# Two attention phases on one core: order tables in pairs of half steps, whole TensorE jobs, and several small steps moved to other engines

## Chip, cores and metric

The kernel runs on one core of a Trainium2 chip. The metric is the device time of one execution in microseconds.

## What is computed

Eight sequences of 512 tokens with 256 features go through two layers. Each layer is an attention half and a feed-forward half, both modulated by a conditioning vector (shift s, scale c, gate g). Cut to what matters here:

```python
# layer 0
h = layernorm(x) * (1 + ca) + sa
q, k, v = h @ wq.T, h @ wk.T, h @ wv.T            # 16 heads of 16 features
q, k = rope(rms(q)), rope(rms(k))                 # per head, g_rms inside rms
y = softmax(q k^T / 4 + 1) v                      # per head
x = x + ga * (y @ wproj.T)
x = x + gb * ffn0(layernorm(x) * (1 + cb) + sb)   # ternary weights, scaled
# layer 1
h = layernorm(x) * (1 + ca) + sa
q, k, v = h @ Wq + bq, h @ Wk + bk, h @ Wv + bv
y = softmax(q k^T / 4) v                          # then normed per head, Wo, gate
x = x + ga * attn(y); x = x + gb * moe(...)       # experts
```

## The kernel before

The program is a row of stages: `setup`, `attention(0)`, `mlp0`, `attention(1)`, `experts`. The change touches `attention` alone. A batch is one sequence. Four heads form a group G, so a batch has four groups.

In `attention` every engine has a program of its own, written out as a loop over half steps `s`, with 64 half steps a batch (`SLOTS`). Each engine runs its instructions strictly in this order and waits on semaphores. Tables (`LAYER_NORM`, `PROJECT`, `ROTATE`, `STACK0`, `STACK1`, `AV_AT`, `STAGE_AT`) say in which half step a step of batch n stands. The steps that prepare batch n stand among the attention of the batches before it; for batches 0 and 1 they stand, in `EARLY0` and `EARLY1`, before the first exponential. Batch n starts at half step 64 n.

Every even half step, TensorE (lines 964 to 980) does two raw score matmuls into the two banks of `SM` (`raw`, 14 pairs ahead) and two score matmuls into one of two buffers `ST` (`scores`). The raw and the score matmuls use different row groups of the array. VectorE (`maximum`, line 678) takes the row maximum of each raw bank. The negated maxima of a group are transposed (job `MT`, line 820), copied by ScalarE (line 496), and put by a DMA of SyncE into the last row of `QS`, so that the exponential needs no other bias. ScalarE (`exponential`, line 487) turns two heads' scores into `P` with one instruction of 128x1024, on every odd half step. A value quarter multiplies `P` with `V`, float32, four heads side by side in 32-column groups of the array (`values`, line 918). A group has four quarters, and each is cut into two halves of 256 columns that stand in different half steps. The sums `AV` are copied to `ysb` (line 560), transposed back into the same bank (line 939), and divided on VectorE (`yn`, lines 708 and 714).

All other TensorE work is a job with the one bank `X`: transposes of the normalised tile (`T0`, `T1`), the projections `QK0` to `QK3`, `V0`, `V1`, transposes of the output (`YT`), in layer 0 the transposes of q and k high and low halves (`H0` to `H3`) and the output projection (`P0`, `P1`). Numbers are split into float16 high and low parts, so that a product takes three matmuls for each half of the features. A `QK`, `V` or `P` job stands in two pieces of two half steps. A job waits until the bank's last content has been read (`job_out`).

Around it, in order of the steps of one batch:

- `STAT`, `AGG` on VectorE give mean and variance. `ve`, `LNG` (logarithm and exponential on ScalarE) and `RSTD` (`refine`, three small VectorE operations) give one over the root. `XN` (line 755, VectorE, four times 128x256) is the normalised tile.
- `T0`, `T1`; ScalarE modulates (line 503) and splits high; GpSimd splits low (line 431).
- Layer 0: after each `QK` job ScalarE copies and squares (lines 511, 514), VectorE sums (`SUM`), and `VAR`, `RMSG`, `INV` give `rr`. VectorE scales `qraw` by it (`UN`, line 780). GpSimd rotates (lines 406 to 416) and forms the low half (line 424). In batch 0 VectorE rotates two of the four tiles. ScalarE forms the high half (line 611) and copies the `H` jobs out of the bank (line 536). SyncE stores and reloads them as `KT` and `QS`.
- Layer 1: the bias enters `QK` and `V` as one more matmul with two rows (lines 837, 846), ScalarE copies (line 520) and splits high, GpSimd low.
- Layer 0 also stages the next stage's weights in 32 parts. GpSimd casts a part (line 384), takes the difference (386), squares it (388) and adds the square to `f_acc` (392), which shows at the end whether any low part is not zero. Parts 0 to 14 come three a batch, parts 15 to 31 one every seven half steps in the last three batches. SyncE loads and stores them.

## Time and profile before

| what | value |
| --- | --- |
| median of 3 runs | 2272.43 us (2268.78 to 2280.82) |
| profiled execution, device time | 2271.84 us |
| its span in the trace | 2270.1 us |
| mean granted TensorE clock | 0.949 of full speed |

The profiled execution lies 0.6 us under the median. Its span starts with the first instruction and ends with the last; 1.7 us lie around it. Times in the trace count from the span's start. PE is TensorE's matmuls, PEld its weight loads, DVE VectorE, ACT ScalarE, POOL GpSimd, SP SyncE. Names with `A_` are tiles of the attention, without the buffer's number. A matmul's length in the trace reaches beyond the start of the next one, so what a matmul occupies is read from start to start.

### The profile page before, as it was taken

The page shows a single profiled execution, that of the slowest core. Times are in us where ns is not written, and L with a number is a line of the kernel's source. Part 1 is how long each engine was busy: PE and PEld are TensorE (multiplying, and loading weights), DVE is VectorE, ACT ScalarE, POOL GpSimd, SP SyncE. Part 2 cuts the span into 40 slices and gives each one's busy share as a digit, 9 for nine tenths or more (in the row PEclk, how much of TensorE's full clock was granted, in tenths as well). Part 3 has the DMA queues.
Part 4 walks back from the last instruction along what each step waited for, and adds up shares of the span by engine and source line. Part 5 has one row for each costly group of instructions (what it writes and reads, how often), then busy time and mean ns, then how long its engine had stood idle before and what let it go on. Part 6 is the DMA issues. An engine that isn't in the chain of part 4 may idle for free. (4 is left out here: it accounts for less than half of the span.)

```text
span 2270.1 us, 33898 instructions
## 1 busy us (share of the span) xinstructions
PE 1951.7 (86%) x12653; PEld 802.8 (35%) x12653; DVE 1397.5 (62%) x2732; ACT 1193.9 (53%) x1686; POOL 593.0 (26%) x510
## 2 busy tenths in 40 slices
PE   4578888999857999999999976999999995688987
PEld 3223333333213444444444431233333332344443
DVE  2478888888814445435435433777777782777672
ACT  1347777777633334234323222577777775556563
POOL 2345655658910000000000002110111100334442
PEclk9999999999987999999999985899999997799999
DMA  3222333335424000000000003333332224322310
GB/s 113 56 56 71 101 83 85 105 98 159 138 76 174 20 1 20 20 1 19 20 9 11 11 33 65 56 66 66 57 60 56 48 37 142 106 102 84 130 36 21
DMA packets 111587, 148.20 MB, mean 65 GB/s; under 512 B 11714, under 2 KB 95027, under 8 KB 109364
## 3 DMA queue, kind: packets, MB, share of 16 engines
q1 hardware_dynamic: 111412, 145.77, 23.3%
q8 instruction: 121, 1.98, 0.4%
q14 instruction: 54, 0.44, 0.1%
HBM read 100.34 MB, written 45.14 MB: 64 GB/s over the span
## 5 line engine op out<-in xcount | busy, mean ns | idle before, releaser
L678 DVE TENSOR_REDUCE A_M<-A_SM 128x1 f16<-128x512 f32 x1024 | 654.2, 687 | 186.8 <-PE A_SM L888 184.4
L487 ACT ACTIVATE A_P<-A_ST 128x1024 f32<-128x1024 f32 x512 | 513.6, 1020 | 67.5 <-PE A_ST L901 67.2
L1256 PE MATMUL B_PA<-B_Hh,B_wh 128*128 128x512 f16 x1024 | 388.1, 379 | 0.0
L1256 PE MATMUL B_PA<-B_Hl,B_wh 128*128 128x512 f16 x1024 | 388.1, 379 | 0.0
L888 PE MATMUL A_SM<-A_KT,A_QS 48*128 48x512 f16 x1024 | 351.3, 400 | 21.5 <-DVE A_M L678 11.4
L918 PE MATMUL A_AV<-A_P,A_V 128*32 128x256 f32 x4096 | 323.0, 393 | 17.9 <-ACT A_P L487 8.9
L1160 ACT ACTIVATE B_af<-B_PA,B_sv 128x512 f32<-128x512 f32 x192 | 132.0, 688 | 357.5 <-PE B_PA L1256 357.4
L901 PE MATMUL A_ST<-A_QS,A_KT 49*128 49x512 f16 x1024 | 302.5, 387 | 1.8 <-DMA A_QS<-A_MT 1.5
L1221 DVE TENSOR_SCALAR B_Hh<-B_af 128x512 f16<-128x512 f32 x128 | 58.0, 453 | 269.6 <-ACT B_af L1160 269.6
L888 PEld LDWEIGHTS A_SM<-A_KT,A_QS 48*128 48x128 f16 x1024 | 75.5, 94 | 303.5 <-DVE A_M L678 253.2
L1116 POOL TENSOR_TENSOR B_hl<-B_hf,B_hh 128x512 f16<-128x512 f32 x16 | 18.5, 1156 | 548.0 <-ACT B_hh L1143 548.0
L918 PEld LDWEIGHTS A_AV<-A_P,A_V 128*32 128x32 f32 x4096 | 85.7, 108 | 174.6 <-issue 123.5
L1256 PEld LDWEIGHTS B_PA<-B_Hl,B_wh 128*128 128x128 f16 x1024 | 100.2, 98 | 119.4
L1256 PEld LDWEIGHTS B_PA<-B_Hh,B_wh 128*128 128x128 f16 x1024 | 100.2, 98 | 119.1
L462 POOL TENSOR_TENSOR A_tr<-A_qkf,A_tr 128x512 f16<-128x512 f32 x32 | 36.9, 1153 | 225.4 <-ACT A_tr L576 225.4
L431 POOL TENSOR_TENSOR A_hl<-A_hf,A_hh 128x512 f16<-128x512 f32 x32 | 37.0, 1156 | 217.0 <-ACT A_hh L551 217.0
L1223 DVE SCALAR_TENSOR_TENSOR B_Hl<-B_af,B_Hh 128x512 f16<-128x512 f32 x128 | 88.6, 693 | 4.4
L802 PE MATMUL A_X<-A_wh,A_hh 128*128 128x256 f16 (+1 forms) x192 | 68.4, 356 | 18.4 <-ACT A_sq L514 14.6
L1215 DVE SCALAR_TENSOR_TENSOR B_uf<-B_PD,B_sv,B_af 128x512 f32<-128x512 f32 x64 | 47.8, 747 | 49.8 <-ACT B_af L1160 26.1
L939 PE MATMUL A_AV<-id,A_ysb 128*128 128x128 f32 x256 | 42.1, 287 | 40.3 <-ACT A_ysb L560 40.0
L825 PE MATMUL A_X<-id,A_xn 128*128 128x128 f32 x128 | 25.8, 336 | 58.8 <-DVE A_xn L755 43.1
L406 POOL TENSOR_TENSOR A_ro<-A_qraw,A_rope 128x512 f32<-128x512 f32 x30 | 41.5, 1382 | 114.7 <-DVE A_qraw L780 104.4
(265 smaller groups left out, 3408.6 us busy)
## 6 DMA issues: line engine op xcount, KB each, us to landing
D_w_st<-in_we_dram SPq DMA_DIRECT2D x16, 1024.0 KB, 5.0
qk<-A_tr SPq DMA_DIRECT2D x62, 256.0 KB, 2.1
A_KT<-qk SPq DMA_DIRECT2D x96, 128.0 KB, 4.4
A_QS<-qk SPq DMA_DIRECT2D x96, 128.0 KB, 4.8
A_w_st<-in_w_ffn_dram SPq DMA_DIRECT2D x32, 352.0 KB, 3.4
w_hi<-A_f_hi SPq DMA_DIRECT2D x32, 176.0 KB, 2.1
w_lo<-A_f_lo SPq DMA_DIRECT2D x32, 176.0 KB, 2.1
B_wl<-w_lo SPq DMA_DIRECT2D x1, 5632.0 KB, 25.0
```

What stands on the lines that cost most here:

```text
L487: nc.scalar.activation(P[:, st, 2 * pair:2 * pair + 2, :], ST[:, u % 2, :, :], ACT.Exp, scale=1.0 / math.sqrt(HD)).then_inc(exp_s, 1)
L678: nc.vector.tensor_reduce(M[G % 2][:, tt, o:o + 1], SM[:, n % 2, :], AX, ALU.max, negate=True).then_inc(max_s, 1)
L802: ins = nc.tensor.matmul(out, a, c, start=first and n_ == 0, stop=last and n_ == len(todo) - 1)
L888: nc.tensor.matmul(SM[:, n % 2, :], QS[b % 2][r, 2 * g + pair, tt * 128:tt * 128 + 128], KT[b % 2][r, 2 * g + pair, :], start=True, stop=T ...
L901: ins = nc.tensor.matmul(ST[:, u % 2, a, :], KT[b % 2][r, pair, o:o + 128], QS[b % 2][r, pair, :], start=True, stop=True)
L918: ins = nc.tensor.matmul(AV[32 * j:32 * j + 32, c_], V[b % 3][:, st, g * HG + j, :], P[:, st, j, c_], start=st == 0 and half == 0, stop=st ...
L939: ins = nc.tensor.transpose(AV[:, tt * 128:tt * 128 + 128], ysb[:, tt * 128:tt * 128 + 128], id32[:, :])
L1160: nc.scalar.activation(af[:, s % 3, :], PA[:, s % 4, :], ACT.Silu if s < HM else ACT.Gelu, scale=sv[:, which, m:m + 1]).then_inc(a_out, 1)
L1215: nc.vector.scalar_tensor_tensor(out=uf[:, s % 2, :], in0=PD[:, s % 2, :], scalar=sv[:, 1, s:s + 1], in1=src, op0=ALU.mult, op1=ALU.mult). ...
L1221: nc.vector.tensor_scalar(Hh[w][:, m, :], src, HS, None, ALU.mult).then_inc(high, 1)
L1223: nc.vector.scalar_tensor_tensor(out=Hl[w][:, m, :], in0=src, scalar=HS, in1=Hh[w][:, m, :], op0=ALU.mult, op1=ALU.subtract).then_inc(spli ...
L1256: ins = nc.tensor.matmul(out, a, c, start=start and kt == 0 and n_ == 0, stop=stop and kt == kts[-1] and n_ == len(ops) - 1)
```

## The change

The tables are written anew in pairs `p` of half steps (32 a batch), and each engine's loop runs over pairs.

- TensorE: `QK`, `V` and `P` jobs and value quarters are no longer cut in two. Quarters stand in pairs 3, 5, 6 and 8 of a group, most jobs in others. `MT` comes after the quarter of its pair.
- ScalarE: `XN` is now an activation with `rstd` as scale and `shift` (minus mean times rstd) as bias. The copy to `ysb` and the emptying of `QK`, `V` and `MT` stand before the pair's exponential, `T` and `YT` behind it in the same pair. The `H` copies leave.
- VectorE: takes over the `H` copies, at the end of a pair. It loses `XN`, the root of LayerNorm, `UN`, `VAR` and `INV` (except in batch 0, where it now rotates all four tiles). It takes one maximum over |low part| of each staged part, ahead of the pair's maxima.
- GpSimd: LayerNorm's root (`norm_root`, eight small operations, one of them a power), for batches from 1 on also `VAR`, `INV` (four small operations) and the scaling, now the first of five operations of `scale_and_rotate`. The square and the sum of the staged parts leave.
- Layer 1: the bias of q and k is added by ScalarE as it empties the bank. V keeps its matmul.
- Staging: four parts in every batch, `f_hi` and `f_lo` with two buffers.

Cut to its core:

```diff
-SLOTS = 64
+PAIRS = 32
+AT0 = placed(-80, dict(STAT=(-51, -48, -45, -43), AGG=-41, ROOT=-40, XN=(-27, -26, -24, -22), T0=-1, T1=1, HH=(0, 2), HL=(1, 3),
+                       QK0=10, QK1=12, QK2=18, QK3=20, V0=26, V1=28, SUM=(12, 14, 20, 22), VAR=(15, 24), RMSG=(16, 26),
+                       INV=(17, 27), ROT=(17, 21, 27, 31), HI=(22, 27, 35, 37), LOW=(24, 28, 36, 38),
+                       H0=39, H1=41, H2=47, H3=49, HIGH=(49, 49, 50, 50, 52, 52, 53, 53), LOWS=(54, 54, 55, 55)))
+AT0 |= OUT | dict(P0=(50,), P1=(52,))
+AT1 = placed(-48, dict(STAT=(-48, -47, -44, -42), AGG=-41, ROOT=-40, XN=(-26, -24, -22, -18), T0=-1, T1=1, HH=(0, 2), HL=(1, 3),
+                       QK0=4, QK1=10, QK2=12, QK3=18, V0=20, V1=26, HIGH=(23, 23, 24, 24, 25, 25, 26, 26), LOWS=(27, 27, 28, 28)))
+EARLY1 = [{}, {}]
+STAGE_AT = [PAIRS * (i // 4) + (20, 22, 25, 27)[i % 4] for i in range(4 * B)]
...
+            def norm_root(n):
+
+                k = 8 * n
+                pool.wait_ge(agg, TT * (n + 1))
...
+                nc.gpsimd.tensor_tensor(lnr[:, 1, :], ve[:, :], power[:, :], ALU.pow).then_inc(root, 1)
...
-            for s in range(BEGIN, END):
+            for p in range(BEGIN, END):
+                n = at(p, "ROOT")
+                if n is not None:
+                    norm_root(n)
...
+                G = group_at(p, 9)
                 if G is not None:
                     act.wait_ge(av_mm, TT * (G + 1))
                     if G >= 1:
                         act.wait_ge(y_mm, G)
                     nc.scalar.activation(ysb[:, :], AV[:, :], ACT.Copy).then_inc(y_cp, 1)
+                if 0 <= p < PAIRS * B:
+                    exponential(p)
...
+                        nc.scalar.activation(xn[:, tt, :], xt[:, tt, :], ACT.Identity, bias=shift[:, tt:tt + 1],
+                                             scale=rstd[:, tt:tt + 1]).then_inc(xn_s, 1)
...
+                    if p - 1 in STAGE_AT:
+                        i = STAGE_AT.index(p - 1)
+                        dve.wait_ge(f_low, i + 1)
+                        nc.vector.tensor_reduce(f_max[:, i:i + 1], f_lo[:, i % 2, :], AX, ALU.max, apply_absolute_value=True
+                                                ).then_inc(f_seen, 1)
+                maximum(2 * p + AHEAD)
+                maximum(2 * p + AHEAD + 1)
+                name, n = jobs.get(p, ("", 0))
+                if name[0:1] == "H":
+                    out_of_bank(name, n)
...
+            for p in range(BEGIN, END):
+                raw(2 * p + AHEAD)
+                if 0 <= p < PAIRS * B:
+                    scores(p, 1)
+                    scores(p, 0)
+                raw(2 * p + AHEAD + 1)
+                name, n = jobs.get(p, ("", 0))
+                if name not in ("", "MT"):
+                    job(name, n)
+                for st, late in enumerate((3, 5, 6, 8)):
+                    G = group_at(p, late)
+                    if G is not None:
+                        values(G, st)
+                if name == "MT":
+                    job(name, n)
```

## Rows read from the trace of the kernel before

**Rows 1.** The page, part 1: busy us (share of the span) and instructions of each engine.

```profile
PE 1951.7 (86%) x12653; PEld 802.8 (35%) x12653; DVE 1397.5 (62%) x2732; ACT 1193.9 (53%) x1686; POOL 593.0 (26%) x510
```

**Rows 2.** Windows: stretch, length, busy (instructions) of five engines, granted clock, DMA share, GB/s.

```profile
33.20:157.60 124.40, 68.14 (x226) 25.62 (x226) 72.76 (x136) 40.93 (x72) 48.38 (x43) 1.00 0.26 63
157.60:488.90 331.30, 295.67 (x2588) 102.00 (x2588) 277.09 (x530) 249.71 (x356) 205.09 (x178) 0.98 0.34 93
356.00:422.50 66.50, 59.23 (x528) 20.57 (x524) 56.02 (x108) 50.42 (x74) 41.50 (x36) 1.00 0.34 97
488.90:652.80 163.90, 146.66 (x1338) 49.21 (x1338) 118.15 (x203) 119.59 (x147) 117.73 (x94) 0.98 0.40 119
1351.70:1431.20 79.50, 46.05 (x133) 13.47 (x133) 35.54 (x66) 19.30 (x31) 21.61 (x16) 0.56 0.31 70
1431.20:1797.90 366.70, 342.20 (x2910) 111.13 (x2908) 284.18 (x555) 264.95 (x369) 41.58 (x36) 0.98 0.31 59
1615.40:1676.20 60.80, 56.69 (x492) 18.63 (x488) 47.49 (x93) 44.41 (x63) 6.92 (x6) 1.00 0.31 62
1797.90:1892.70 94.80, 90.14 (x839) 30.18 (x839) 69.12 (x122) 75.56 (x96) 2.31 (x2) 1.00 0.20 35
```

**Rows 3.** Timeline of TensorE in a steady batch of layer 1: start, length, instruction.

```profile
1621.37 0.39 PE L837 MATMUL A_X<-A_ones,A_b 2*128 2x512 f16 x1
1621.69 0.39 PE L802 MATMUL A_X<-A_hh,A_wh 128*128 128x512 f16 x1
1621.91 0.38 PE L802 MATMUL A_X<-A_hl,A_wh 128*128 128x512 f16 x1
...
1623.55 0.39 PE L802 MATMUL A_X<-A_hh,A_wh 128*128 128x512 f16 x1
...
1624.30 0.64 PE L918 MATMUL A_AV<-A_P,A_V 128*32 128x256 f32 x8
1624.88 0.39 PE L888 MATMUL A_SM<-A_KT,A_QS 48*128 48x512 f16 x1
```

**Rows 4.** The same timeline, the transposes of the attention output; idle time in brackets.

```profile
1618.39 0.66 PE L939 MATMUL A_AV<-id,A_ysb 128*128 128x128 f32 x4 [0.86 <-ACT A_ysb L560]
```

**Rows 5.** Groups, VectorE, one steady batch of layer 0: busy us, mean ns, idle before.

```profile
L678 DVE TENSOR_REDUCE A_M<-A_SM 128x1 f16<-128x512 f32 x64 | 41.0, 686 | 7.8 <-PE A_SM L888 7.8
L780 DVE TENSOR_TENSOR A_qraw<-A_qraw,A_rr 128x512 f32<-128x512 f32 x5 | 3.5, 707 | 0.1
L755 DVE TENSOR_SCALAR A_xn<-A_xt,A_mv,A_rstd 128x256 f32<-128x256 f32 x4 | 3.2, 830 | 0.0
...
L740 DVE TENSOR_SCALAR A_ve<-A_mv 128x4 f32<-128x4 f32 x1 | 0.2, 170 | 0.0
```

**Rows 6.** Groups, ScalarE, the same batch of layer 0.

```profile
L536 ACT ACTIVATE A_tr<-A_X 128x1024 f16<-128x1024 f16 x4 | 4.2, 1062 | 0.0
```

**Rows 7.** Groups, VectorE, one steady batch of layer 1.

```profile
L755 DVE TENSOR_SCALAR A_xn<-A_xt,A_mv,A_rstd 128x256 f32<-128x256 f32 x4 | 1.6, 409 | 0.0
```

**Rows 8.** Groups, ScalarE, the same batch of layer 1.

```profile
L567 ACT ACTIVATE A_ysq<-A_yn 128x256 f32<-128x256 f32 x4 | 1.6, 398 | 0.0
```

**Rows 9.** Groups, GpSimd, one steady batch of layer 0.

```profile
L406 POOL TENSOR_TENSOR A_ro<-A_qraw,A_rope 128x512 f32<-128x512 f32 x4 | 5.5, 1368 | 11.5 <-DVE A_qraw L780 11.3
...
L392 POOL TENSOR_TENSOR A_f_acc<-A_f_acc,A_w_st 128x704 f32<-128x704 f32 x3 | 5.1, 1687 | 0.2
...
L388 POOL TENSOR_TENSOR A_w_st<-A_f_lo 128x704 f32<-128x704 f16 x3 | 4.1, 1359 | 0.2
```

**Rows 10.** Groups, GpSimd, the stage after the two attention phases.

```profile
L1527 POOL TENSOR_TENSOR D_r<-D_ve,D_power 128x4 f32<-128x4 f32 x16 | 16.2, 1015 | 65.3 <-DVE D_ve L1728 65.3
```

**Rows 11.** Timeline of VectorE early in layer 0.

```profile
50.19 5.80 DVE L740 TENSOR_SCALAR A_ve<-A_mv 128x4 f32<-128x4 f32 x1
```

**Rows 12.** Timeline of TensorE before the first raw scores of layer 0.

```profile
126.98 1.09 PE L825 MATMUL A_X<-id,A_xn 128*128 128x128 f32 x4 [10.36 <-DVE A_xn L755]
```

**Rows 13.** Waits of TensorE in the last batch of layer 0: us, times, longest.

```profile
PE A_X L802 <- POOL A_yTl L452: 7.2, 1, 7.2
```

More of the change, by code:

```diff
@@ L782, in _ @@
-                    for tt in range(TT):
-                        n = at(s, "ROT", tt)
-                        if n is not None and by_dve(n, tt):
+                    if p - 1 in STAGE_AT:
[4 more added lines that the diff above has]
+                maximum(2 * p + AHEAD)
```

514 lines of the change are left out of this document (251 added, 263 removed).

## The prediction

> **What bounds the kernel now.** I read the busy totals first [rows 1]. TensorE is busy for 86% of the span, but that is a mean over stages, and the change touches only the two attention phases. So I cut the trace at the start of the first exponential of each batch and read busy time by stretch [rows 2]. Layer 0 takes 124.4 us before its first exponential, then 331.3 us for five batches (66.5 us each once steady) and 163.9 us for the last three. Layer 1 takes 79.5 us, then 366.7 us for six batches (60.8 us each once steady) and 94.8 us for the last two. The reader is to see that in a steady batch of layer 1 TensorE is busy 56.7 of 60.8 us, VectorE 47.5 and ScalarE 44.4. In layer 0 they are busy 59.2, 56.0 and 50.4 of 66.5 us, and GpSimd 41.5. No engine has much room, and they are tied to each other: SM has two banks, so a raw score matmul waits for the maximum taken two before it, and ST has two, so scores wait for the exponential two pairs back. A pair therefore lasts about as long as the longest of its three engine shares. The dear pairs set the batch, and emptying one engine alone doesn't.
>
> **TensorE, part by part.** The trace shows what a cut costs. A QK piece of three matmuls starts at 1623.55 and what follows it starts at 1624.30. That is 0.75 us for three matmuls, and a step from one such matmul to the next is 0.22 (1621.69 to 1621.91), so a block pays about 0.1 us beyond its steps [rows 3]. Half a value quarter takes 0.58 us (1624.30 to 1624.88). I take 0.14 us saved for each pair of halves joined, a little above the 0.1 of the QK piece since its matmuls are float32 (bounds: nothing, and 0.2). With 16 quarters that is 2.2 us a batch. Joined jobs (four QK and two V, in layer 0 two P as well) save 6 to 8 times 0.1 us. Layer 1 also loses the bias matmul of each QK job: 1621.37 to 1621.69, 0.32 us, four times, 1.3 us. The sum is 4.1 us a batch in layer 1 and 3.0 in layer 0.
>
> The transposes of the attention output wait 0.86 us for ysb [rows 4], because ScalarE runs that copy after an exponential. The new order puts it ahead of the exponential and directly behind the last quarter. The wait is then the copy plus its handoffs less the scores that go in between, about 0.4 us by my estimate. Four times 0.46 is 1.8 us a batch. The bias on ScalarE costs nothing there: it rides on a copy that exists.
>
> That makes 60.8 - 4.1 - 1.8 = 54.9, say 55 us for layer 1, and 66.5 - 3.0 - 1.8 = 61.7, say 61.5 us for layer 0, if nothing else becomes late.
>
> **What could be late: VectorE.** In layer 0 it loses the normalised tile (4 x 0.83 = 3.3 us) and the scaling by rr (4 x 0.707 = 2.8 us) [rows 5]. It also loses the small operations of three roots: 14 of them at about 0.2 us (the one on four columns takes 0.17), 2.8 us. It gains four copies of H out of the bank, 128x1024 float16. The trace has no such copy on VectorE. The maximum over 512 columns of the same kind of bank takes 0.686 us, so twice that, 1.37, is the upper end and 0.69 the lower. The same copy takes 1.06 us on ScalarE [rows 6]. I take 1.2, nearest to VectorE's own row at full length. It also gains four maxima over 704 columns, 0.686 x 704/512 = 0.94 us each. So 56.0 - 8.9 + 4.8 + 3.8 = 55.7 us, under 61.5. A pair with a copy and a staged maximum holds 2 x 0.69 + 1.2 + 0.94 = 3.5 us. There VectorE is last, and TensorE waits for a bank; I let that offset any gain below 61.5. In layer 1 it only loses work: 47.5 - 1.6 for the tile [rows 7] - 0.8 for the root.
>
> **ScalarE.** In layer 0 it loses four copies of H (4.2 us) and gains four tiles of 256 columns, 0.40 us each by its square of that size [rows 8]. In layer 1 it gains 1.6 and loses 0.4: 45.6 of 55. The tiles are spread over four pairs.
>
> **GpSimd.** Each part of the weight staging loses its square and its sum, 1.36 + 1.69 us [rows 9]. In steady batches there were three parts, 9.2 us less; a fourth comes, and its cast and difference I put at 2.4 us, so -6.8. Scaling is added, four times 1.37 by the rope product of that shape, 5.5 us. The three roots add 18 small operations. The nearest row is a power of 128x4, 1.01 us [rows 10]; the others do less arithmetic on as few columns, so I take 0.2 each, and 1.01 for the one power, 4.4 us (1 to 18 us at the bounds). 41.5 - 6.8 + 5.5 + 4.4 = 44.6 us, of 61.5. It fits on average. In place it is tight: behind a rotation with its scaling (four times 1.37, about 5.4 us) stand the later low halves and the staging, and VectorE, in order, waits for f_low at the top of the next pair, with its two maxima queued behind. TensorE waits for those. The low half of the last tile goes ahead of the second part, so I expect waits of 1 to 2 us twice a batch, of which the slack of 6 us in VectorE pays most.
>
> Here a rule of the skill weighs in. With GpSimd filling its tiles, a VectorE operation on four columns lasts 5.80 us [rows 11] where in a steady batch it takes 0.17, and the normalised tile takes 0.83 us in layer 0 against 0.41 in layer 1, where GpSimd is nearly idle [rows 5, 7]. By the Trainium skill, page "SBUF — State Buffer", section "Who interferes with whom", a VectorE operation in a two-port mode and a GpSimd operation lock each other out for a whole instruction, and a tensor_reduce never contends; the trace agrees. By it, what stays on VectorE is not stretched by the work moved to GpSimd.
>
> **Before the first exponential.** In layer 0, TensorE sits idle for 10.4 us until the tile of the third batch is there [rows 12]. That tile was held up on VectorE behind the four-column chain under GpSimd. On ScalarE, with its root computed early on GpSimd, it is ready in time. The 5.80 us hold also goes from the path of the first QK. Against it, all four rotations of batch 1 now carry their scaling on GpSimd, 5.4 us each, and the H transposes stand early in TensorE's queue. Of some 16 us I keep 12 (5 to 18). In layer 1 the same hold goes and so do four bias matmuls, but the root of the second batch stands ahead of the low half of the first on GpSimd: 4 us (0 to 8).
>
> **The ends of the layers.** The last three batches of layer 0 stage 17 parts in a row. In the last one TensorE waits 7.2 us in one place for GpSimd's yTl [rows 13]. With four parts a batch this goes. The three batches average 54.6 us. I take 56 for the first (its preparation ends half-way, and it takes over copies and maxima), 49 for the second and 43.3 for the third, since the last two of layer 1, without staging, average 47.4. So 163.9 becomes 148.3. The last two of layer 1 go from 94.8 to 88 by quarters and waits.
>
> **Sum.** 12 + (331.3 - 5 x 61.5 = 23.8) + 15.6 + 4 + (366.7 - 56 - 5 x 55 = 35.7) + 6.8 = 97.9 us, off the 2271.84 us of the profiled execution: 2173.9. The median is 0.6 us above that execution, so 2174.
>
> **Rivals.**
> *Starved banks (20%).* A whole QK job holds TensorE for 1.4 us and a whole quarter for 1.0, without a raw score between. VectorE, with two banks, runs dry and then has its own 1.4 us ahead of it. It is idle 13 us of a batch in layer 1 now. For: both idle times are real. Against: jobs move to pairs without a quarter. If the merges' gain is so given back and only waits, prologue and ends remain, that is 11 x 1.8 + 12 + 15.6 + 4 = 51 us: 2221.
> *Cheaper copies (10%).* If the H copy takes 0.69 us, 2 us leave VectorE in each batch just where it is last, and the staging waits are hidden by slack: 11 batches gain 2 us more, 2152. By the Trainium skill, page "VectorE: DVE Perf Modes", section "The perf-mode tier table (the rule you actually need)", a copy from PSUM can run at up to twice the rate; no row here shows a float16 one.
> *Slower: VectorE waits for GpSimd (8%).* The maximum of a staged part stands ahead of the pair's maxima. If a whole rotation of 5.4 us is still ahead of f_low in GpSimd's queue, the six batches with preparation have 24 such waits, 130 us, and the time is 2174 + 130 = 2304. It decides from 97.9 / 24 = 4.1 us a wait. For: GpSimd's chain is nearly unbroken through more than half of the batch. Against: the parts stand behind the last rotation, not amid them.
> *Nothing moves (5%).* The moved work may be late by as much as the merges save, in every batch: 2272. My forecast keeps 57%, 2140 to 2205 on its own. So 57 + 20 + 10 = 87% faster, 5% the same and 8% slower; 0.5% is about what a measurement of this kernel can tell from no change.
>
> The range takes in both ends of the copies, the prologues and the starved case: 2130 to 2235.
>
> **What would show it.** Steady batches of 61.5 and 55 us; a whole value quarter of about 1.0 us and a QK job of about 1.4; the wait for ysb at 0.4 us; no wait for yTl of several us in the last batch; the first raw score of layer 0 at about 113 us in place of 128. Wrong if VectorE's maximum of a staged part waits over 4 us, if VectorE's idle time in layer 1 stays at 13 us, or if the granted clock of 1.00 in steady batches [rows 2] is lower.

## The result and the profile after

The changed kernel takes 2243.3 us (median of 4 runs, 2241.1 to 2244.6) beside 2272.25 us before: ratio 0.9866, 95% interval 0.9837 to 0.9895. That is 29 us faster, where I forecast 98. Its profiled execution has a span of 2242.9 us. Cut at the same places as [rows 2], by the starts of the first exponential of each batch:

| stretch, us | before | forecast | changed kernel | last kernel of the study |
|---|---|---|---|---|
| start to first exponential, layer 0 | 157.6 | 145.6 | 159.0 | 153.6 |
| layer 0, five batches | 331.3 | 307.5 | 308.6 | 296.4 |
| layer 0, last three | 163.9 | 148.3 | 162.8 | 152.5 |
| last exponential of layer 0 to first of layer 1 | 778.4 | 774.4 | 778.3 | 776.7 |
| layer 1, six batches | 366.7 | 331.0 | 357.9 | 334.7 |
| layer 1, last two | 94.8 | 88.0 | 97.5 | 94.4 |

The miss of 69 us lies in three places: 27 us in the six batches of layer 1, 24 in the ends of the two layers, 17 in the two openings. Only the five batches of layer 0 came out as forecast.

The page of the changed kernel, busy totals and granted clock in 40 slices:

```profile
PE 1893.0 (84%) x10573; PEld 776.7 (35%) x10573; DVE 1352.3 (60%) x2590; ACT 1212.8 (54%) x1686; POOL 577.0 (26%) x668
PEclk9769999999968999999999986999999996799999
```

Windows of the changed kernel, columns as in [rows 2]:

```profile
33.20:159.00 125.80, 59.70 (x224) 23.78 (x224) 54.35 (x117) 40.09 (x73) 60.96 (x84) 0.73 0.26 63
159.00:467.60 308.60, 287.45 (x1948) 97.23 (x1948) 262.00 (x461) 244.46 (x341) 211.36 (x260) 0.95 0.45 109
283.70:345.20 61.50, 57.70 (x397) 19.75 (x396) 53.09 (x96) 49.68 (x70) 43.24 (x54) 0.97 0.47 117
467.60:630.40 162.80, 141.73 (x966) 42.44 (x964) 127.64 (x213) 118.81 (x145) 60.38 (x63) 0.98 0.37 97
1408.70:1766.60 357.90, 320.45 (x2117) 104.55 (x2116) 271.61 (x498) 282.63 (x376) 54.11 (x76) 0.95 0.32 59
1711.20:1766.60 55.40, 51.49 (x357) 17.30 (x357) 44.06 (x77) 45.85 (x60) 6.96 (x6) 1.00 0.33 58
1766.60:1864.10 97.50, 84.89 (x592) 25.68 (x591) 70.21 (x125) 77.56 (x95) 1.15 (x1) 1.00 0.18 34
```

In [rows 2] the granted clock was 0.98 to 1.00 in these stretches; now it is 0.95 in both loops, and 0.73 in the opening of layer 0, where e13 tests what it costs. The sixth batch of layer 1 (1711.2 on) takes the 55 us of the forecast at a clock of 1.00, the five before it 58.9, 62.3, 61.0, 59.6 and 60.6. All six have nearly the same work on TensorE (357 matmuls in the sixth as in a steady batch of e1), but only the first five load, measure and normalise a tile for a later batch. The timeline at the start of the second batch shows it (SyncE's issue, then VectorE and TensorE; idle time in brackets):

```profile
1466.72 0.37 SPq L314 DMA_DIRECT2D A_xt<-x_tok  x1
...
1472.00 0.43 DVE L780 BATCH_NORM_STATS2 A_st<-A_xt 128x6 f32<-128x256 f32 x1 [4.17 <-DMA A_xt<-x_tok]
1472.34 1.27 DVE L733 TENSOR_REDUCE A_M<-A_SM 128x1 f16<-128x512 f32 x2
...
1473.07 0.60 PE L920 MATMUL A_SM<-A_KT,A_QS 48*128 48x512 f16 x1 [4.13 <-DVE A_M L733]
```

SyncE issues the load when the last part of the tile before has been normalised. The statistics stand one pair later on VectorE, with the pair's maxima behind them; in the tables of the kernel before, 50 half steps (25 pairs) lay between. TensorE waits for those maxima, and its raw score takes 0.60 us afterwards in place of 0.39. That is the lower level, 1.2 GHz: the granted clock is 0.57 from 1472 to 1478.

In layer 0 the staged part shows in VectorE's groups of the batch at 283.7 (compare [rows 5]), with the new copy below it:

```profile
L803 DVE TENSOR_REDUCE A_f_max<-A_f_lo 128x1 f32<-128x704 f16 x4 | 3.5, 880 | 2.0 <-POOL A_f_lo L394 2.0
L750 DVE COPY A_tr<-A_X 128x1024 f16<-128x1024 f16 x5 | 3.4, 679 | 0.0
```

The same load holds up the opening of layer 0. There it brings the tile of the fourth batch, and its statistics stand two pairs behind it:

```profile
99.80 0.43 SPq L314 DMA_DIRECT2D A_xt<-in_x_tok_dram  x1
...
108.82 0.43 DVE L780 BATCH_NORM_STATS2 A_st<-A_xt 128x6 f32<-128x256 f32 x1 [12.01 <-DMA A_xt<-in_x_tok_dram]
...
111.77 0.61 PE L841 MATMUL A_X<-A_wh,A_hh 128*128 128x512 f16 x1 [8.96 <-ACT A_sq L554]
```

VectorE stops for 12.0 us with a sum of squares of batch 1 queued behind; a small GpSimd operation waits for that sum, ScalarE for both, and TensorE for ScalarE. This QK job starts 11.7 us behind the one before it (100.06); in the kernel before the same step takes 3.9 (98.70 to 102.62). No run of the study takes this wait away.

And later in the opening, where [rows 12] had the idle 10.4 us:

```profile
122.86 1.04 POOL L415 TENSOR_TENSOR A_lnr<-A_ve,A_power 128x4 f32<-128x4 f32 x1
...
125.59 1.15 POOL L453 TENSOR_TENSOR A_qkl<-A_qo,A_qkh 128x512 f16<-128x512 f32 x1
126.83 0.24 POOL L476 TENSOR_SCALAR A_rv<-A_rv 128x64 f32<-128x64 f32 x1
127.11 0.26 ACT L644 ACTIVATE A_rln<-A_rv 128x64 f32<-128x64 f32 x1 [9.02 <-POOL A_rv L476]
...
128.19 0.40 PE L841 MATMUL A_X<-A_wh,A_hh 128*128 128x256 f16 x1 [9.76 <-ACT A_V L569]
```

The small operation of 0.24 us at 126.83 stood on GpSimd behind two rotations, a root and a low half. ScalarE waited for it with the copy of V queued behind, and TensorE for that copy.

### The profile page after: what moved, and what is told of

Read it like the earlier page. It is cut to its first block and busy times, and to the rows that moved or that the text cites. A ratio compares the mean times of both kernels' runs of the same rounds, so it can differ in the third digit from the quotient of the medians.

```text
span 2242.9 us, 29738 instructions
## 1 busy us (share of the span) xinstructions
PE 1893.0 (84%) x10573; PEld 776.7 (35%) x10573; DVE 1352.3 (60%) x2590; ACT 1212.8 (54%) x1686; POOL 577.0 (26%) x668
## 5 line engine op out<-in xcount | busy, mean ns | idle before, releaser
L527 ACT ACTIVATE A_P<-A_ST 128x1024 f32<-128x1024 f32 x512 | 523.0, 1024 | 140.4 <-PE A_ST L933 137.8
L920 PE MATMUL A_SM<-A_KT,A_QS 48*128 48x512 f16 x1024 | 358.1, 404 | 89.8 <-DVE A_M L733 78.7
L933 PE MATMUL A_ST<-A_QS,A_KT 49*128 49x512 f16 x1024 | 307.3, 394 | 0.2
L948 PE MATMUL A_AV<-A_P,A_V 128*32 128x512 f32 x2048 | 279.7, 619 | 5.9 <-ACT A_P L527 5.0
L920 PEld LDWEIGHTS A_SM<-A_KT,A_QS 48*128 48x128 f16 x1024 | 81.7, 94 | 429.0 <-DVE A_M L733 360.0
L948 PEld LDWEIGHTS A_AV<-A_P,A_V 128*32 128x32 f32 x2048 | 40.7, 109 | 85.3 <-issue 70.7
L780 DVE BATCH_NORM_STATS2 A_st<-A_xt 128x6 f32<-128x256 f32 x64 | 25.0, 416 | 74.4 <-DMA A_xt<-x_tok 50.0
L841 PE MATMUL A_X<-A_wl,A_hh 128*128 128x256 f16 (+1 forms) x192 | 65.2, 339 | 0.0
L841 PE MATMUL A_X<-A_wh,A_hl 128*128 128x256 f16 (+1 forms) x192 | 65.2, 339 | 0.0
```

The lines of the kernel that those rows point to most:

```text
L527: nc.scalar.activation(P[:, st, 2 * pair:2 * pair + 2, :], ST[:, u % 2, :, :], ACT.Exp, scale=1.0 / math.sqrt(HD)).then_inc(exp_s, 1)
L841: ins = nc.tensor.matmul(out, a, c, start=first and n_ == 0, stop=last and n_ == len(todo) - 1)
L920: nc.tensor.matmul(SM[:, n % 2, :], QS[b % 2][r, 2 * g + pair, tt * 128:tt * 128 + 128], KT[b % 2][r, 2 * g + pair, :], start=True, stop=T ...
L933: ins = nc.tensor.matmul(ST[:, u % 2, a, :], KT[b % 2][r, pair, o:o + 128], QS[b % 2][r, pair, :], start=True, stop=True)
L948: ins = nc.tensor.matmul(AV[32 * j:32 * j + 32, :], V[b % 3][:, st, g * HG + j, :], P[:, st, j, :], start=st == 0, stop=st == TT - 1)
```

## The experiments

Times are medians of 4 or 5 runs; ratios are to the kernel before, measured beside it on the same chip. Kernels e1 to e4 start from the changed kernel, e5 to e7 and e9 to e17 from e8. Five groups ran on one chip each: e1 to e4, e5 to e8, e9 to e12, e13 to e16, and e17 with e18. The kernel before had medians of 2267.5, 2272.2, 2270.6, 2270.6 and 2269.5 us there, so a difference of under 5 us between kernels of two groups shows nothing by itself.

| kernel | edit | us | ratio, 95% |
|---|---|---|---|
| e1 | statistics of layer 1 later | 2220.4 | 0.9798 (0.9782 to 0.9814) |
| e2 | staged maximum later | 2227.8 | 0.9824 (0.9804 to 0.9844) |
| e3 | small operation off GpSimd | 2242.2 | 0.9881 (0.9865 to 0.9898) |
| e4 | e3 and another order of the opening | 2239.0 | 0.9873 (0.9856 to 0.9889) |
| e8 | e1, e2 and e4 | 2198.7 | 0.9687 (0.9654 to 0.9719) |
| e5 | quarters cut, halves adjacent | 2199.5 | 0.9689 (0.9664 to 0.9715) |
| e6 | a bias matmul put back | 2208.3 | 0.9724 (0.9698 to 0.9750) |
| e7 | tile on VectorE | 2209.4 | 0.9734 (0.9708 to 0.9760) |
| e9 | quarters cut, halves in two pairs | 2221.6 | 0.9782 (0.9760 to 0.9804) |
| e10 | ysb behind the exponential | 2294.7 | 1.0105 (1.0065 to 1.0144) |
| e11 | as e9, halves amid the pair | 2304.8 | 1.0155 (1.0130 to 1.0180) |
| e12 | jobs cut amid the pair | 2227.6 | 0.9810 (0.9788 to 0.9833) |
| e13 | filler in the openings | 2195.3 | 0.9662 (0.9639 to 0.9684) |
| e14 | halves in light batches only | 2191.2 | 0.9652 (0.9632 to 0.9673) |
| e15 | tile of three batches on VectorE | 2197.9 | 0.9681 (0.9661 to 0.9701) |
| e16 | H copies on ScalarE | 2200.4 | 0.9688 (0.9666 to 0.9711) |
| e17 | e14 and the last H copies on ScalarE | 2186.7 | 0.9640 (0.9619 to 0.9660) |
| e18 | the changed kernel again | 2247.0 | 0.9899 (0.9879 to 0.9918) |

### The load of the next tile

```
-AT1 = placed(-48, dict(STAT=(-48, -47, -44, -42), AGG=-41, ROOT=-40, ...
+AT1 = placed(-48, dict(STAT=(-43, -42, -39, -37), AGG=-36, ROOT=-35, ...
```

> Only layer 1's table is changed: the statistics of the next batch's tile stand five pairs later (STAT=(-43, -42, -39, -37), AGG=-36, ROOT=-35), so six pairs behind the load of that tile and not one. My theory: in the changed kernel layer 1 misses its forecast because SyncE starts the load of the next tile only when ScalarE has normalised the last quarter of the one before, and VectorE asks for that tile one pair later, ahead of two maxima; VectorE sits 50 us waiting for the load over the phase, pair 0 of a batch lasts 3.5 to 6.5 us, and the granted clock falls behind it. The one batch with full preparation but no reload (the sixth) lasts 55.5 us. By this the first five batches of layer 1 go from 58.9, 62.3, 61.0, 59.6 and 60.6 us to about 55.5 each, the clock is 1.00 in them, and the time falls by 23 to 27 us, to 2217 or so. Rival, that these pairs are dear for another reason (the engines have no room, and the wait only takes up slack of the last pairs): the wait goes and another comes in its place, batches stay over 59 us and the time falls by less than 6 us.

Measured: the batches of layer 1 take 56.8 and then 55.5 us each, and the phase from first to last exponential is 432.8 us in place of 455.4. The time is 21.8 us below e3's, which ran beside it and differs from the changed kernel by next to nothing; I had expected 23 to 27. Windows of e1, the first six batches and one of them:

```profile
1406.90:1741.00 334.10, 309.98 (x2117) 102.99 (x2117) 271.27 (x498) 281.92 (x377) 54.11 (x76) 0.99 0.34 64
1519.10:1574.60 55.50, 51.59 (x357) 17.40 (x357) 45.68 (x86) 47.54 (x66) 9.43 (x14) 1.00 0.36 68
```

TensorE has the same 2117 matmuls as in the changed kernel, busy for 310 us and not 320: that is the clock. VectorE's waits for the load were 14.0 us in all in the changed kernel (five, the longest 4.2), and not the 50 that I had written. The stretch lost 24 us, so the slower clock behind each wait cost about as much again as two thirds of the wait. The theory holds and its rival falls.

### The staged maximum

```
-                    if p - 1 in STAGE_AT:
-                        i = STAGE_AT.index(p - 1)
+                    if p - 3 in STAGE_AT:
+                        i = STAGE_AT.index(p - 3)
```

> Only the place of the maximum over a staged weight part is changed: three pairs behind the part and not one. In the changed kernel VectorE waits 2.1 us a batch for f_low there, pairs 21 and 22 last 3.2 us each, and TensorE's clock falls just behind them. If that wait is worth what it shows and a little of the clock, layer 0 has six batches that gain 1.5 to 2.5 us each: 9 to 15 us in all. Rival, that VectorE's slack and the work that is bunched there (low halves, copies of H) set those pairs anyway: under 4 us.

Measured: layer 0 takes 455.1 us from first to last exponential in place of 471.4, 16.3 less; the five batches 295.3 in place of 308.6, and the seventh batch 53.5 in place of 57.3. Waits of VectorE from the second to the fifth batch, the changed kernel first, then e2:

```profile
DVE A_M L733 <- PE A_SM L920: 19.0, 34, 1.2
DVE A_f_max L803 <- POOL A_f_lo L394: 7.7, 8, 1.3
```

```profile
DVE A_M L733 <- PE A_SM L920: 18.6, 34, 1.2
```

Eight waits of about 1 us went, and next to nothing came in their place (0.6 us for the load of a tile). One wait for f_low stays in either kernel, in the eighth batch: 3.4 us in the changed one, 3.7 in e2. The gain is somewhat more than I expected; the granted clock of the five batches rose from 0.95 to 0.99.

### The opening of layer 0

e3 gives the small operation of batch 1 back to VectorE (`if n in (0, 1)` there, `if n and n > 1` on GpSimd).

> The mean squares of batch 1 are scaled on VectorE again, as those of batch 0 are (one small operation a half), so that they no longer stand behind two rotations, a root and a low half in GpSimd's queue. In the changed kernel ScalarE waits 9.0 us for that operation at 127.1 us with the copy of V queued behind it, and TensorE sits idle 9.8 us for that copy; the first raw score starts at 133.7. Theory 1: the wait on the queue goes and the first raw score starts at about 124, but TensorE then waits in pair -9 for the features of batch 1, whose last rotation GpSimd still ends at about 140; so the first exponential (159.0) moves by less than 2 us and the time by less than 2. Rival: the wait for the small operation alone is what delays the opening, and the first exponential comes 8 to 10 us earlier, with the time.

Measured: the first raw score comes at 126.9 us in place of 133.7, the first exponential at 157.9 in place of 159.0. TensorE then waits 5.4 us for the rotated features of batch 1. Theory 1 holds: the visible wait was not the bound.

```
+          | placed(-48, dict(ROT=(17, 21, 27, 35), HI=(22, 27, 36, 39), LOW=(24, 28, 37, 40), H0=47, H1=48, H2=49, H3=53,
+                             HIGH=(54, 54, 55, 55, 56, 56, 57, 57), LOWS=(58, 58, 59, 59)))]
```

> As the kernel with the scaling of batch 1 on VectorE, and besides the last rotation of batch 1, its high and low halves, the four transposes of its features and their loads stand later (the transposes at pairs -1, 0, 1 and 5 in place of -9, -7, -1 and 1), so that the low half of the third batch's tile goes ahead of that rotation on GpSimd. If GpSimd's order, and not its speed, is what takes the gain that I forecast for the opening of layer 0 (12 us), the first exponential comes at 148 to 152 us in place of 159.0 and the time falls by 7 to 11 us. If GpSimd is the bound with its whole work (four rotations of 5 us, a root of 3, the halves), something in the first batch waits in its place and the time falls by less than 3 us.

Measured: first raw score at 124.3, first exponential at 151.9, at the late end of what I expected. The time falls by 3.2 us against e3, between my two outcomes and within the spread of e3's runs (2236.8 to 2242.5): in the traces the first batch lasts 64.9 us in place of e3's 63.6, and the sixth and seventh together 2.4 us more. With this order the first exponential comes at 151.7 to 154.7 us in the later kernels, e7 apart. So order explains 4 to 7 of the 13 us missing here, and about 4 of those are lost again in e4 by the end of the layer.

e13 asks whether TensorE's clock holds the rest:

```
+                for _ in range(FILL.get((name, n), 0)):
+                    nc.tensor.matmul(AV[:, :], wh[:, 0, 0:128], wh[:, 0, 0:T], start=True, stop=True)
```

> On top of the kernel with all three moves: while TensorE waits in the openings of both layers it runs filler matmuls (128 rows, 512 columns, into the bank of the attention output, which nothing reads yet): 2 to 4 in each short gap, 7 to 24 in the long ones. They change nothing in the output. In the opening of layer 0 the granted clock is 0.5 from about 80 us on in the changed kernel and 1.00 in the kernel before, but a QK job of six matmuls takes 2.74 us in both, which is the time at 1.2 GHz, not the 1.4 of a steady batch. If the missing gain of the opening is the clock, the QK jobs fall to 1.4 us and the first exponential of layer 0 comes 5 us or more earlier (154.2 in the kernel without filler), and that of layer 1 some us too. If the chain through the engines' queues sets the opening, it moves by less than 3 us, or later by the filler's own time.

Windows from 84 to 102 us, e8 first, then e13:

```profile
84.00:102.00 18.00, 11.76 (x50) 5.28 (x50) 3.45 (x5) 5.55 (x10) 4.15 (x9) 0.50 0.75 132
```

```profile
84.00:102.00 18.00, 14.28 (x86) 6.39 (x84) 3.45 (x5) 5.49 (x10) 4.50 (x9) 1.00 0.76 141
```

The clock stayed up there and a QK matmul of batch 1 took 0.38 us in place of 0.61. Yet the first exponential comes at 151.7, where e4, e8, e14 and e15 with the same order of the opening have 151.9 to 154.2, and the one of layer 1 comes no earlier behind layer 0's last (776.8 us against 777.6). So the miss there isn't the clock's. The faster jobs run into the load of the fourth tile, for which VectorE waits 12.3 us in e13 and 11.9 in e8.

> On top of the kernel with all three moves: the normalised tiles of the first three batches of layer 0 are made on VectorE, all others on ScalarE. With all tiles on VectorE the first exponential came at 148.9 us and not at 154.2, while three steady batches were 2.3 us longer. If the gain in the opening belongs to the tile, the first exponential comes at about 149 and the time falls by 4 to 5 us. If it was the clock of that one execution (granted 1.00 for longer), the first exponential comes anywhere from 149 to 154 and the median falls by less than 2 us.

Measured: first exponential 151.9, time 0.8 us lower, within the noise, so the 148.9 of e7 does not belong to those three tiles. What does follow it is the load: the statistics of the fourth tile start at 105.4 us in e7, 106.2 in e15, 106.5 in e4 and 108.5 in e8, and the first exponential comes at 148.9, 151.9, 151.9 and 154.2. In all fourteen kernels with e4's order it comes 43.6 to 46.4 us behind that start.

### What joining earned

e5 cuts each quarter into two blocks of 256 columns directly behind each other.

> On top of the kernel with all three moves: each value quarter is again two blocks of four matmuls over 256 columns, in the same pair and behind the same wait. My term: joined halves save 0.14 us a quarter (bounds 0 and 0.2), and it is on the path in every pair, so 256 quarters make it slower by 36 us (51 at the upper bound), some 2.2 us a batch. Rival: a pair with a quarter has slack on TensorE behind VectorE's maxima, and less than 10 us come back.

Measured: 2199.5 against 2198.7, and each steady pair is as long as before to 0.01 us. My term isn't a property of the block.

```
-                for st, late in enumerate((3, 5, 6, 8)):
+                for st, lates in enumerate(((3, 4), (5, 6), (6, 7), (8, 9))):
```

> On top of the kernel with all three moves: the value quarters are halves in neighbouring pairs again, one half a pair and in one pair of eight two, each at the end of its pair, and the copy of the output, its transposes and what follows stand one pair later, as in the kernel before. Two halves directly behind each other cost nothing (steady batch of layer 1 55.5 us either way), so what joining earned, if anything, is the boundary to the raw scores between them. My term, 0.14 us a quarter: 2.2 us a batch, 57.7 us in layer 1, 36 us in all. Rival 1: there is no such boundary cost and nothing changes, under 5 us. Rival 2: whole quarters bunch TensorE's work in four pairs of eight while VectorE runs dry, so the halves are faster where no other work is in the batch; the last two batches of layer 1 go from 97.5 us back towards the 94.8 of the kernel before.

The kernel also runs the copy of the output, its transposes and what follows one pair later, since the last half stands there.

Measured: 22.9 us slower. Windows of a steady batch of layer 1 in e8, then of one in e9 and of e9's last two:

```profile
1556.20:1611.70 55.50, 51.58 (x357) 17.41 (x357) 45.66 (x86) 47.53 (x65) 9.44 (x14) 1.00 0.35 68
1576.00:1634.10 58.10, 55.50 (x485) 20.37 (x484) 45.42 (x86) 47.88 (x66) 9.47 (x14) 1.00 0.35 65
1749.70:1844.10 94.40, 89.13 (x843) 32.00 (x847) 70.06 (x124) 76.62 (x95) 1.16 (x1) 1.00 0.18 35
```

A steady batch is 2.6 us longer than e8's 55.5, and one of layer 0 3.0 to 4.1; the term was 2.2. TensorE is busy 3.9 us longer, 0.24 a quarter, where e5 with its adjacent halves has e8's 51.6; its waits fall from 3.8 to 2.5 us, though 1.4 of these are new: for VectorE's division, which reads the later output. But the last two batches take 94.4 and not 97.5, in layer 0 97.1 and not 100.9. The size of the term and rival 2 both hold, each in its place. e14 takes the one without the other:

> On top of the kernel with all three moves: in the last two batches of each layer, where TensorE has no projection left, the value quarters are halves in neighbouring pairs again; in the first six they stay whole. With halves everywhere these four batches took 52.3, 44.8, 52.0 and 42.3 us, with whole quarters 54.8, 46.1, 53.6 and 43.9. If whole quarters starve VectorE there (the part of my term for the ends that failed), the time falls by 6 to 7 us and no other batch changes. If it was something else that changed with the halves (the later copy of the output), less than 2 us.

Measured: 7.5 us faster. The four batches take 52.9, 44.8, 52.0 and 42.3 us, the others what they took. Here too the copy of the output stands a pair later in these batches, so the run doesn't tell it from the halves, as I had expected it to. The waits speak for the halves: in the seventh batch of layer 1 TensorE waits 5.0 us for maxima in e8 and not at all in e14, and 0.5 and 0.2 us for ysb. Layer 1, last two batches of e14:

```profile
1718.10:1770.10 52.00, 50.18 (x459) 18.53 (x459) 43.84 (x77) 40.63 (x50) 1.15 (x1) 1.00 0.30 52
1770.10:1812.50 42.40, 38.81 (x385) 13.58 (x389) 26.26 (x48) 36.02 (x45) 0.00 (x0) 1.00 0.04 14
```

e6 puts `nc.tensor.matmul(X[:, :], b2[:, 0:128], ones2[:, :], start=True, stop=True)` ahead of each QK job of layer 1.

> On top of the kernel with all three moves: in layer 1 each of the four QK jobs of a batch begins again with a matmul of two rows and 512 columns, as the bias was, whose result the product then overwrites; so the output is the same and only TensorE's time comes back. My term: 0.32 us a job, 32 jobs, 10 us, all of it on the path, 1.3 us a batch (0.22 a job, 7 us, by the step from one matmul to the next). Rival: such a matmul is hidden in part, under 4 us.

Measured: 9.6 us slower, each of the four pairs 0.31 to 0.32 us longer in a steady batch. This term was exact.

> On top of the kernel with all three moves: each QK and V job is cut in two blocks, the first ahead of the pair's second raw score and the second behind it, in the same pair. The rival of starved banks says that VectorE runs dry during a whole job of 1.4 us: then the cut gives back some 0.5 us in each of six pairs, 3 us a batch, 30 us in all faster. My term says that a block costs 0.1 us at its boundary: six times 0.1, 0.6 us a batch, 9 us in all slower. If a pair with a job is TensorE's and a boundary costs nothing, under 3 us.

Measured: 28.9 us slower, outside all three. The pair of V0 goes from 2.73 to 3.05 us, that of QK0 from 2.20 to 2.62. A QK job whole in e8, then a QK job's second half behind a raw score of its own in e12:

```profile
1558.84 0.39 PE L923 MATMUL A_SM<-A_KT,A_QS 48*128 48x512 f16 x1
1558.84 0.60 PE L936 MATMUL A_ST<-A_QS,A_KT 49*128 49x512 f16 x2
1559.24 0.39 PE L923 MATMUL A_SM<-A_KT,A_QS 48*128 48x512 f16 x1
1559.56 0.39 PE L844 MATMUL A_X<-A_hh,A_wh 128*128 128x512 f16 x1
...
1560.96 0.39 PE L923 MATMUL A_SM<-A_KT,A_QS 48*128 48x512 f16 x1
1560.96 0.60 PE L936 MATMUL A_ST<-A_QS,A_KT 49*128 49x512 f16 x2
1561.19 0.38 PE L923 MATMUL A_SM<-A_KT,A_QS 48*128 48x512 f16 x1
1561.49 1.06 PE L951 MATMUL A_AV<-A_P,A_V 128*32 128x512 f32 x8
1562.38 0.39 PE L861 MATMUL A_X<-id,A_M 128*4 128x128 f16 x4
```

```profile
1579.83 0.39 PE L924 MATMUL A_SM<-A_KT,A_QS 48*128 48x512 f16 x1
1580.15 0.39 PE L844 MATMUL A_X<-A_hh,A_wh 128*128 128x512 f16 x1
```

In e8 a raw score and a score start at the same 1558.84, and the block of four at 1560.96 is over in 0.53 us. A raw score cut off from its score runs alone and takes 0.31 to 0.32 us of its own. So this edit measured the loss of an overlap, not my boundary of 0.1.

> As the kernel with the quarters in halves in neighbouring pairs, but each half stands between the scores and the second raw score of its pair, so that the two raw scores of a pair are further apart. If VectorE is starved between the pairs because both raw scores come in one block, its idle time (11 us in a steady batch of layer 1) falls by 2 us a batch or more against the kernel with the halves at the end, and the time by 15 us or more. If TensorE's own work sets those pairs, the order within the pair changes the time by less than 5 us either way.

Measured: 83 us slower than e9; a steady batch of layer 1 takes 62.5 us. It tears the same overlap in nearly every pair. It says nothing of starved banks.

### The copy of the output

```
-                G = group_at(p, 9)
-                if G is not None:
...
-                    nc.scalar.activation(ysb[:, :], AV[:, :], ACT.Copy).then_inc(y_cp, 1)
                 if 0 <= p < PAIRS * B:
                     exponential(p)
+                G = group_at(p, 9)
+                if G is not None:
...
+                    nc.scalar.activation(ysb[:, :], AV[:, :], ACT.Copy).then_inc(y_cp, 1)
```

> On top of the kernel with all three moves: ScalarE copies the attention output out of its bank behind the pair's exponential again, not ahead of it. My term: TensorE's transposes, which now wait 0.18 us for the copy, wait some 0.5 us longer, four times a batch, 1.8 us a batch and 29 us in all; the steady batch of layer 1 goes from 55.5 to 57.3. Upper bound, a whole exponential of 1.02 us each time: 4.1 us a batch, 65 us. Rival: that wait lies in slack of TensorE in that pair (VectorE's maxima are last there), under 8 us in all.

Measured: 96 us slower, beyond my upper bound of 65. A steady batch of layer 1 takes 61.6 us. Waits of TensorE in it, and the timeline where one ends:

```profile
PE A_AV L974 <- ACT A_ysb L597: 5.2, 4, 1.6
```

```profile
1549.27 0.65 PE L974 MATMUL A_AV<-id,A_ysb 128*128 128x128 f32 x4 [1.60 <-ACT A_ysb L597]
```

TensorE waits up to 1.6 us four times a batch, and the granted clock of the batch is 0.97. In the changed kernel the wait is 0.2 us, 0.4 a batch where the profile shows any; the kernel before had 0.86 at a time [rows 4] and 3.2 us a batch. This is no undoing of the change, since the kernel before ran the copy at another place; it shows how much hangs on that place.

### What was moved between engines

e7 makes the tile on VectorE in both layers, with `nc.vector.tensor_scalar(xn[:, tt, :], xt[:, tt, :], rstd[...], shift[...], ALU.mult, ALU.add)` at the same pairs.

> On top of the kernel with all three moves: the normalised tile is made on VectorE again (one multiply and add a quarter by the same shift and root from GpSimd, at the same pairs, ahead of the two maxima), in both layers. By my sums VectorE gains 1.6 us a batch in layer 1 and 1.6 to 3.3 in layer 0, ScalarE loses 2.4. If VectorE is last in the pairs where the tile stands, batches last 1 to 3 us longer, 10 to 40 us in all, and moving the tile to ScalarE earned that. Rival: the pairs where the tile stands are TensorE's or ScalarE's, and the time changes by less than 5 us either way.

Measured: 10.7 us slower. The second to fourth batch of layer 0 are 2.1 to 2.6 us longer (61.6 to 61.9 against 59.0 to 59.8), some 7 us in all, and the steady batches of layer 1 are the same, 55.5. The stretch between the layers is 5.2 us longer, but it is 4.7 longer in e16 too, whose edit touches nothing there, so I don't count it for the tile. The tile on VectorE in e7, first in layer 0, then in layer 1:

```profile
L805 DVE TENSOR_SCALAR A_xn<-A_xt,A_rstd,A_shift 128x256 f32<-128x256 f32 x4 | 3.2, 809 | 0.0
```

```profile
L805 DVE TENSOR_SCALAR A_xn<-A_xt,A_rstd,A_shift 128x256 f32<-128x256 f32 x4 | 1.6, 405 | 0.0
```

In the steady batches the move earned its time in layer 0 alone. The maxima take the same time in both layers, the tile twice as long where GpSimd is busy, as in [rows 5, 7]. By the Trainium skill, page "SBUF — State Buffer", section "Who interferes with whom", a reduction (tensor_reduce) never contends with GpSimd and a two-port mode does; the trace agrees, with 0.68 to 0.69 us for the maxima in both layers and 0.81 against 0.41 for the tile.

> On top of the kernel with all three moves: the four copies of the transposed features of a batch go out of their bank on ScalarE again (1.06 us each), behind the exponential, and not on VectorE, where they take 0.69 us. If VectorE is last in these pairs, the batches of layer 0 get shorter by up to 0.6 us a copy, 2.4 us a batch. If ScalarE's place behind the exponential holds TensorE's next job or the maxima are not last, they get longer by 1 to 4 us a batch, 6 to 24 us in all; I take this as the likelier, since the copy of the output behind its exponential cost 6 us a batch.

Measured: 1.7 us slower, within the noise and under the 6 to 24 that I took as likelier. The first five batches together are 3.5 us longer, the sixth and seventh 1.7 and 2.7 us shorter (56.3 and 52.1). A copy takes 1.03 us on ScalarE, 0.68 on VectorE.

### The parts together

> The three moves together: statistics of layer 1 later, the staged maximum later, and the opening of layer 0 in the other order. Alone they moved their phases, by the traces, by 22.6 us (layer 1, first to last exponential), 16.3 us (layer 0, first to last exponential), and 7.1 us (first exponential of layer 0), of which 4 came back as longer batches with waits for the staged part. If the causes are separate places, the sum is 22.6 + 16.3 + 7.1 = 46 us, and 42 if the 4 us are lost again: 2197 to 2201 by the changed kernel's 2243. If GpSimd's or TensorE's work bounds the whole, less than 35.

Measured: 2198.7 us, 44.6 below the changed kernel's first measurement, as the separate causes add up to.

> The three moves, halves of quarters apart in the last two batches of each layer, and the four feature copies of the last batch of layer 0 on ScalarE, where the sixth and seventh batch have room on it. With halves alone the time was 2191.2 us; with all feature copies on ScalarE the sixth and seventh batch of layer 0 took 56.3 and 52.1 us in place of 58.0 and 54.8, the others 0.3 to 0.9 longer. If both hold together, 2188 to 2190 us, ratio to the kernel before 0.963 to 0.965. If the light halves already took that room, 2191.

> The changed kernel itself, beside the kernel above on the same chip: 2243 us, ratio 0.987 to the kernel before. The moves of the kernel above are then worth 52 to 55 us; of the 69 us by which the forecast of 2174 missed, 14 to 17 stay.

Measured: 2186.7 and 2247.0 us on one chip, 60.3 us apart; e17 has a ratio of 0.964 to the kernel before, and lies 1.3 us under the 2188 to 2190 expected. Windows of e17, by the stretches of the table:

```profile
153.60:450.00 296.40, 280.52 (x2600) 117.21 (x2598) 261.80 (x463) 243.19 (x342) 211.52 (x260) 0.99 0.47 116
450.00:602.50 152.50, 142.51 (x1345) 53.27 (x1348) 125.44 (x210) 121.42 (x149) 61.01 (x63) 1.00 0.40 105
1379.20:1713.90 334.70, 310.78 (x2878) 127.64 (x2877) 271.53 (x498) 281.91 (x377) 54.07 (x76) 0.99 0.34 64
```

## Why the prediction was right or wrong

**Layer 1, six batches: 331 forecast, 357.9 measured.** The step that failed is the part "What could be late". It looked for VectorE's waits on GpSimd and sized its work in layer 1, but it left out SyncE's load of the tile, which follows the end of the normalisation. The new table puts that end one pair ahead of the next statistics, where 25 pairs had lain between. The moved step brings its DMA along, and the reader stops for it. With that taken away the stretch is 334.1 us, 3 above the forecast. No rival held this either.

**Layer 1's terms.** The bias: 1.3 us a batch forecast, 1.25 measured (e6). Quarters: 2.2 forecast, 2.6 measured, but for a whole quarter as against halves in two pairs with a later output copy (e9); my reason, a price for a block wherever it stands, is refuted by e5. The wait for ysb: 0.86 to 0.4 forecast; 0.2 measured, 2.8 us a batch where I had 1.8. The tile: no effect (e7); on ScalarE a part of it takes 0.59 us where I had 0.40. The three terms together are 6.7 us and the batch fell by 5.3, so some 1.4 us and the gain of the joined jobs are given back, and no run tells where. Those jobs could not be cut without tearing the overlap, so their term stays open.

**Layer 0, five batches: 307.5 forecast, 308.6 measured.** Right as a sum, not as an argument. I put the wait for f_low at 1 to 2 us twice a batch and let VectorE's slack pay most of it. It measured 1 us twice a batch and was paid in full: 2.7 us a batch by e2, with the clock behind it. TensorE's side was as much better, 58.6 to 59.6 us a batch without the wait where I had 61.7: quarters some 3.6 us (2.2 forecast), the tile off VectorE (2.1 to 2.6 by e7, which I had put at nothing as long as TensorE is last) and the shorter wait for ysb. The rival in which VectorE's waits make it slower needed 4.1 us in each of 24 waits; twelve show in the layer's trace, 14.7 us in all, the longest 1.3 in the steady batches and 3.4 in the eighth. The H copy is at the low bound, 0.68 us and not 1.2. By the Trainium skill, page "VectorE: DVE Perf Modes", section "The perf-mode tier table (the rule you actually need)", a copy from PSUM can run at up to twice the rate; the trace agrees: 0.68 us for 1024 float16 columns, where the maximum over 512 float32 columns takes 0.69. But the rival that hung on it gave the batch 2 us for it, and e16 shows that the place of the copy moves the whole time by less than 2 us.

**Ends of the layers: 236.3 forecast, 260.3 measured.** The yTl wait of [rows 13] is gone, as foreseen. The term failed in three ways. For layer 0 I took the last two batches of layer 1 as the model, though its three batches still carry staging, copies and the end of the preparation: 59.3, 57.3 and 46.1 us against my 56, 49 and 43.3. I let the merges gain in batches that have few jobs or none: there, by the waits in e8 and e14, whole quarters leave VectorE dry in turn, which is the starved-banks rival, at 1.3 to 2.5 us in each of four batches (e9, e14; the later output copy isn't separated). I had that mechanism and placed it in full batches, where it is not last. And I took 1.8 us a batch for the shorter wait for ysb there: with the halves back, the last two batches of layer 1 take 94.4 us, where the kernel before has 94.8 and I had 88, so nothing of that gain shows, and no run tells why. The seventh and eighth batch of layer 0 together further lost 2.5 us to the staged wait (103.4 against 100.9 in e2).

**Openings: 16 us forecast, 1.3 us lost.** The 10.4 us of [rows 12] went as I said, and 9.8 us came at a job ahead of it in TensorE's order, for another reason. I wrote that GpSimd's rotations carry their scaling and took 4 of some 16 us off for it, but followed nothing of what stands behind them in its queue. e3 shows that even this wait hid another one, e4 that the order costs 4 to 7 us of the opening. For the 6 to 9 us that stay missing the trace shows the step left out in layer 1 too, the load of a tile: it holds VectorE for 12.0 us and makes a QK job of batch 1 7.8 us late (11.7 us behind its forerunner in place of 3.9). That the first exponential moves with this load (e7, e15, e4, e8) speaks for it; no run took the wait away, so its worth is not measured. In layer 1 neither the 4 us nor anything else appeared, and I didn't test why.

**What I said would show it.** The whole quarter takes 1.00 us from its start to the next raw score (1734.76 to 1735.76), the QK job 1.40 (1559.56 to 1560.96): right. Steady batches of 61.5 and 55: right for layer 0 and for the one undisturbed batch of layer 1. First raw score at 113: wrong, 133.7. Of the signs against me, no staged maximum waited over 4 us, but VectorE's idle time in layer 1 did stay, at 14.4 us a batch over the first six (9.8 in a steady batch of e8). The granted clock stayed at 1.00 only there where nothing stalled; I had named its fall too, and it was a sign: of the 44.6 us that e8 gained, a part is TensorE at 1.2 GHz behind waits of 1 to 4 us.

**Size.** Of the 69 us missing, e17 finds 57 by its median against 2243.3 and 60 against 2247.0 beside it. It stays 12.7 us above the forecast.

## What to carry to other kernels

When a step moves, to another engine or in the order, move its DMA in the sum too: ask when the buffer is reloaded and how many steps later the first reader stands, for the reader's engine stops with all that is queued behind. Join work where the engine is full and cut it finely where it is not; the same merge (with the output copy a pair earlier) earned 2.6 us in one batch and lost 1.6 in another. When a forecast meets the time, still undo its terms one by one, since two errors of 2.5 us a batch had hidden each other here.

## What the hardware showed unexpectedly

- A raw score over 48 rows and a score over 49 rows start at the same time (1558.84 above), and four such matmuls take 0.53 us where four of 128 rows step by 0.22 each; a raw score that stands alone costs 0.31 to 0.32 us (1579.83 to 1580.15). Only the cuts of e11 and e12 made that visible.
- A wait of 4.1 us of TensorE behind a dense stretch was followed by matmuls of 0.60 us in place of 0.39, at a granted clock of 0.57 over the next 6 us and 0.86 over the 6 after those; the wait cost about two thirds more than itself.
- A granted clock of 1.00 doesn't say that matmuls run at 2.4 GHz. In the opening of the kernel before it was 1.00 throughout, and a QK matmul still took 0.61 us. It took 0.38 in e13, where filler ran in the gaps:

```profile
94.78 0.61 PE L802 MATMUL A_X<-A_wh,A_hh 128*128 128x512 f16 x1 [1.12 <-ACT A_P L536]
95.18 0.63 PE L802 MATMUL A_X<-A_wl,A_hh 128*128 128x512 f16 x1
```
